# A routed block on one core: the last token tile's router chain put between chunks of expert tiles, and expert tiles that add to the output without waiting for their neighbour

## What is computed

```
t  = tokens(x + involution(layernorm_channels(x)))          # 12544 x 128
n  = layernorm(t)
p, e = top_k(softmax(n @ router_w.T), 2);  p = p / (sum(p) + 1e-9)     # 8 experts, 2 per token
y  = sum over the token's two experts of  p * (silu(n @ w1[e].T) * (n @ w3[e].T)) @ w2[e].T   # hidden 341
out = t + y
```

## Time and profile before

| | |
|---|---|
| median of 3 runs | 1515.86 us (1513.18 to 1517.63) |
| profiled execution | 1514.45 us, its span 1512.6 us |
| busy in the span | PE 1300.8 us, DVE 1074.7, POOL 830.7, ACT 415.9 |
| mean granted TensorE clock | 0.969 of full speed |

### The profile page before, as it was taken

One profiled execution on the slowest core, in us unless ns is written; L12 is line 12 of the kernel. 1 busy time (PEld: TensorE's weight loads), 2 busy tenths in 40 slices (PEclk: granted clock), 3 DMA queues, 4 the chain that ended last, 5 costly groups with the idle time before them and its releaser, 6 DMA issues.

```text
span 1512.6 us, 25000 instructions
## 1 busy us (share of the span) xinstructions
PE 1300.8 (86%) x8596; PEld 1127.5 (75%) x8596; DVE 1074.7 (71%) x2247; ACT 415.9 (27%) x1055; POOL 830.7 (55%) x573
## 2 busy tenths in 40 slices
PE   0598988899999999999999999999999999848871
PEld 0387777788888888888888878888788888737661
DVE  2599899887877878778777887778878778422220
ACT  2112020322323223232232323323232131423330
POOL 1233535357475564756647566475664747464454
PEclk9999999999999999999999999999999999988996
DMA  5001010333334343333433434334333333456662
GB/s 145 13 1 37 20 43 23 88 74 99 74 88 94 74 101 73 86 94 76 99 78 82 96 74 98 79 81 102 67 87 85 83 81 78 108 116 149 147 132 36
DMA packets 91230, 123.37 MB, mean 82 GB/s; under 512 B 13042, under 2 KB 68466, under 8 KB 91104
## 3 DMA queue, kind: packets, MB, share of 16 engines
q1 hardware_dynamic: 54592, 94.95, 21.9%
q0 software_dynamic: 36512, 26.83, 13.0%
HBM read 87.17 MB, written 34.56 MB: 80 GB/s over the span
## 4 chain that ended last, share of the span: by engine, by line
PE 60%; DVE 14%; issue 8%; DMA 7%; ACT 6%; POOL 3%; SPq 1%; POOLq 0%; DVEq 0%; ACTq 0%
PE acc_ps L390 22%; PE kern_ps L468 15%; DVE prod L853 8%; PE bank L500 7%; DMA out<-y_sb,xs 5%; PE hid_ps L492 5%; PE hid_ps L491 5%; PE bank L390 3%; DVE stats_ln L723 3%; POOL out L983 3%; PE bank L421 2%; PE bank L448 1%; ACT L632 1%; DVE x_res L860 1%; ACT rows L583 1%
## 5 line engine op out<-in xcount | busy, mean ns | idle before, releaser
L853 DVE TENSOR_TENSOR prod<-kern_ps,xn 128x896 f32<-128x896 f32 x686 | 733.2, 1084 | 77.8 <-PE kern_ps L468 72.0
L468 PE MATMUL kern_ps<-h_stack,span 98*128 98x448 f32 x1372 | 477.1, 431 | 85.0 <-DVE prod L853 82.7
L390 PE MATMUL acc_ps<-consts_sb,prod 128*128 128x128 f32 x3920 | 545.7, 276 | 0.0
L983 POOL DMA_INDIRECT out<-y_sb,xs x210 | 330.2, 1572 | 335.3 <-ACT y_sb L645 245.1
L390 PEld LDWEIGHTS acc_ps<-consts_sb,prod 128*128 128x128 f32 x3920 | 471.6, 143 | 51.9 <-issue 12.0
L992 POOL TENSOR_TENSOR prod<-prod 128x896 f32<-128x896 f32 x126 | 270.3, 2146 | 183.5 <-DVE prod L853 182.5
L468 PEld LDWEIGHTS kern_ps<-h_stack,span 98*128 98x128 f32 x1372 | 227.9, 194 | 136.8 <-DVE prod L853 120.1
L971 POOL DMA_INDIRECT sorted_x<-rows,dst x196 | 190.7, 973 | 68.3 <-issue 53.7
L632 ACT ACTIVATE silu<-hid_ps 114x256 f32<-114x256 f32 x228 | 87.3, 383 | 418.4 <-PE hid_ps L492 418.2
L873 DVE TENSOR_TENSOR hid<-hid_ps,silu 114x256 f32<-114x256 f32 x228 | 96.2, 422 | 103.0 <-ACT silu L632 102.9
L491 PE MATMUL hid_ps<-xc,w_sb 128*114 128x256 f32 x456 | 137.5, 383 | 1.3
(11 more groups left out here) (93 smaller groups left out, 939.2 us busy)
## 6 DMA issues: line engine op xcount, KB each, us to landing
w_sb<-in_w SPq DMA_DIRECT2D x105, 342.0 KB
w_sb<-in_w SPq DMA_DIRECT2D x105, 192.0 KB, 2.4
xs<-sorted_x SPq DMA_DIRECT2D x105, 130.0 KB, 2.1
x_ln<-in_x SPq DMA_DIRECT2D x14, 448.0 KB, 3.8
x_res<-in_x SPq DMA_DIRECT2D x14, 448.0 KB, 3.5
out<-x_res SPq DMA_DIRECT2D x14, 448.0 KB, 2.5
out<-y_sb,xs POOLq DMA_INDIRECT x210
sorted_x<-rows,dst POOLq DMA_INDIRECT x196, 2.4
```

Source lines behind the costliest of these rows:

```text
L390: return mm(dst, lhsT=src, rhs=eye, is_transpose=True, start=start, stop=True, skip_group_check=True)
L468: i = mm(kern_ps[:, n % 2, h, 0:HALF], span[:, u * C:(u + 1) * C], h_stack[:, m % 2, h * HALF:(h + 1) * HALF], start=True, stop=True)
L853: v.tensor_tensor(tiled(prod[:, n % PRING, :].rearrange("p (h n) -> p h n", h=2)), tiled(kern_ps[:, n % 2, :, 0:HALF]), window(m, u // KS, ...
L983: g.indirect_dma_start(out[:, :], bass.IndirectOffsetOnAxis(ap=xs[:, j % XBUFS, b, C:C + 1].bitcast(U32), axis=0), y_sb[:, j % YBUFS, b, : ...
```

## The change

It has four parts.

1. **Adds.** The counter of landed adds is split in two, by the parity of the tile. In the last stage a tile waits for its neighbour's adds only where the expert changes (or for tiles of no expert), and always for the adds of the tile before that. DVE computes which (`needs`, 3 instructions); POOL reads the number to wait for into a register.
2. **The last tile's chain.** Its normalising, transposes, logits, rank and router steps move forward and are spread over the chunks of tiles 77 to 80; its 14 sends are split 6, 4, 4 behind tiles 78, 79 and 80 in place of 7, 7 behind 78 and 79; SP writes the pads before it waits for the sends; tile 77's loads go ahead of the store of the last residual tile.
3. **The router steps of all tiles** get another order: mask first, then everything that needs the ranks up to `dst`, then the gates. In the slots beside the taps: the exponential goes from u = 20 to u = 25, step 6 (places) to u = 24, `hot_place`, which multiplies two SBUF operands, to u = 25, the cast to `dst` to u = 26, the gates to u = 26 to 28, the table steps to u = 29 to 35, and the sends to u = 29 to 48 (before: 27 to 47). PE may take the shared bank after step 8, not after step 17.
4. **Buffers**: 7 of rows, 5 of `y_sb`, 3 of each weight set.

```
-XBUFS, YBUFS = 6, 4
+XBUFS, YBUFS, WBUFS = 7, 5, 3
...
+        def added(j):
+
+            return 16 * TB * (j // 2 + 1)
...
# load_expert (SP)
-                    for i in (m - 1, m):
-                        sp.wait_ge(s_rows[i % 2], 16 * 2 * NB * (i // 2 + 1))
                     if m == TILES - 1:
                         for e in range(EXPERTS):
...
                         sp.wait_ge(s_pads, 16 * (EXPERTS + 2))
+                    for i in (m - 1, m):
+                        sp.wait_ge(s_rows[i % 2], 16 * 2 * NB * (i // 2 + 1))
...
             load_expert(BESIDE)
+            load_expert(BESIDE + 1)
             store_x1(TILES - 1)
...
# take_bank, rank (PE)
                 elif last == "rank":
-                    pe.wait_ge(s_rt, RT * r + 18)
+                    pe.wait_ge(s_rt, RT * r + 9)
...
# PE after the taps
+                    if (i, c) in ((1, 2), (2, 0)):
+                        channels_of_x1(last, int(i == 2))
+                    if (i, c) == (2, 1):
+                        logits(last)
+                    if (i, c) == (3, 1):
+                        rank(last)
...
# ACT beside the taps
-                    if u == 20:
-                        exponentials(m - 1)
...
+                if u == 25 and 0 <= m - 1:
+                    exponentials(m - 1)
...
# DVE: new step 8 is cnt, 9 hot_place, 10 dst_f, 11 dst, 12 rows<-tok, 13 total (waits for the exponential)
-                    for k in {17: (0,), 18: (1,), 19: (2, 3), 20: (4, 5), 21: (6, 7), 22: (8, 9), 23: (10, 11),
-                              24: (12, 13), 25: (14, 15), 26: (16, 17, 18)}.get(u, ()):
+                    for k in {17: (0,), 18: (1,), 19: (2, 3), 20: (4,), 21: (5,), 24: (6, 7), 25: (8, 9, 10), 26: (11, 12, 13),
+                              27: (14, 15), 28: (16, 17, 18)}.get(u, ()):
...
# DVE after the taps
+                    for k in {(2, 1): (0,), (2, 2): (1, 2), (3, 0): (3, 4, 5), (3, 1): (6, 7, 8, 9, 10, 11),
+                              (3, 2): (12, 13, 14, 15, 16, 17, 18)}.get((i, c), ()):
+                        router_step(last, k)
...
# send (POOL)
-                    pool.wait_ge(s_rt, RT * m + 16)
+                    pool.wait_ge(s_rt, RT * m + 18)
...
# add_to_out (POOL)
-                    if j:
-                        pool.wait_ge(s_added, 16 * TB * j)
+                    if j > stage_tiles(TILES - 1)[0]:
+                        if j == stage_tiles(TILES - 1)[0] + 1:
+                            pool.wait_ge(s_need, 1)
+                        enough = pool.value_load(need_i[0:1, j:j + 1], min_val=added(j - 3), max_val=added(j - 1))
+                        pool.wait_ge(s_added[(j - 1) % 2], enough)
+                        pool.sem_inc(s_enough, 1)
+                    elif j:
+                        pool.wait_ge(s_added[(j - 1) % 2], added(j - 1))
+                    if j >= 2:
+                        pool.wait_ge(s_added[j % 2], added(j - 2))
```

More of the change, by code:

```diff
@@ L231, in build @@
         pad_i = sb("pad_i", [P, EXPERTS], I32)
+        same = sb("same", [P, most])
+        need_i = sb("need_i", [P, FTILES], I32)
         hid = sb("hid", [HC, 2, CPE, T])
@@ L272, in build @@
         s_xs = [sem(f"s_xs{i}") for i in range(XBUFS)]
-        s_w13 = [sem(f"s_w13_{i}") for i in range(2)]
-        s_w2 = [sem(f"s_w2_{i}") for i in range(2)]
+        s_w13 = [sem(f"s_w13_{i}") for i in range(WBUFS)]
+        s_w2 = [sem(f"s_w2_{i}") for i in range(WBUFS)]
         s_xt = sem("s_xt")
@@ L281, in build @@
         s_yout = sem("s_yout")
-        s_added = sem("s_added")
+        s_added = [sem(f"s_added{i}") for i in range(2)]
+        s_need = sem("s_need")
+        s_same = sem("s_same")
+        s_enough = sem("s_enough")
         NCONST = 6
@@ L377, in _ @@
             load_expert(BESIDE)
+            load_expert(BESIDE + 1)
             store_x1(TILES - 1)
-            for j in range(BESIDE + 1, FTILES):
+            for j in range(BESIDE + 2, FTILES):
                 load_expert(j)
@@ L500, in down @@
                         i = mm(dst[:, b * C:(b + 1) * C], hid[:, j % 2, c, b * P:(b + 1) * P],
-                               w2_sb[0:HC, j % 2, c * C:(c + 1) * C], start=b == 0 and c == 0, stop=c == CPE - 1,
+                               w2_sb[0:HC, j % WBUFS, c * C:(c + 1) * C], start=b == 0 and c == 0, stop=c == CPE - 1,
                                skip_group_check=True)
@@ L689, in _ @@
                     q = CPE * i + c
+                    if (i, c) == (1, 0):
+                        norm_x1(last, 0)
                     silus(j, c, kern_ps[:, q % 4 // 2, q % 2, :])
@@ L765, in router_step @@
                 elif k == 5:
-                    i = v.tensor_tensor(mask[:], hot[:, :, 0, :], hot[:, :, 1, :], ALU.add)
+                    i = v.tensor_tensor(diff[:], top[:], top[:, :, 0:1].broadcast_to([P, NB, EXPERTS]), ALU.subtract)
                 elif k == 6:
+                    i = v.tensor_tensor(place[:], lg, repeated(offset[:], 1, NB), ALU.add)
+                elif k == 7:
+                    i = v.tensor_tensor(offset[:], offset[:], bank[:, GT:GT + EXPERTS], ALU.add)
+                elif k == 8:
+                    i = v.tensor_tensor(cnt[:], cnt[:], bank[:, GT:GT + EXPERTS], ALU.add)
+                elif k == 9:
+                    i = v.tensor_tensor(hot_place[:], hot[:], place[:].unsqueeze(2).broadcast_to(each), ALU.mult)
+                elif k == 10:
+                    i = v.tensor_reduce(dst_f[:], hot_place[:], AX, ALU.add)
+                elif k == 11:
+                    i = v.tensor_copy(dst[:, m % 2], dst_f[:])
+                elif k == 12:
@@ L775, in router_step @@
                     i = v.tensor_tensor(gden[:], gden[:], expd[:, :, 0], ALU.add)
-                elif k == 10:
+                elif k == 16:
                     i = v.reciprocal(grec[:], gden[:])
-                elif k == 11:
+                elif k == 17:
                     i = v.tensor_tensor(rows[:, m % 2, :, :, C + 1], expd[:, :, 0:2].rearrange("p b k -> p k b"),
                                         repeated(grec[:], 1, 2), ALU.mult)
[L781 to L792, removed]
@@ L838, in table_step, with needs @@
                 i.then_inc(s_cnt, 1)
+            def needs():
+                a, b = stage_tiles(TILES - 1)
+                q = b - a - 1
+                dve.wait_ge(s_cnt, TS * (TILES - 1))
+                v.tensor_tensor(same[:, 0:q], expert_f[:, 1:q + 1], expert_f[:, 0:q], ALU.is_equal).then_inc(s_same, 1)
+                dve.wait_ge(s_same, 1)
+                v.scalar_tensor_tensor(out=same[:, 0:q], in0=expert_f[:, 1:q + 1], scalar=float(EXPERTS), in1=same[:, 0:q],
+                                       op0=ALU.is_lt, op1=ALU.mult).then_inc(s_same, 1)
+                dve.wait_ge(s_same, 2)
+                v.scalar_tensor_tensor(out=need_i[:, a + 1:b], in0=same[:, 0:q], scalar=-16.0 * TB, in1=need_c,
+                                       op0=ALU.mult, op1=ALU.add).then_inc(s_need, 1)
             def product(n):
@@ L933, in _ @@
                         ln("ln2", last, 3, None, None)
-                    if i == 3:
-                        for k in ((0, 1, 2), (3, 4, 5, 6), (7, 8, 9, 10, 11))[c]:
-                            router_step(last, k)
+                    for k in {(2, 1): (0,), (2, 2): (1, 2), (3, 0): (3, 4, 5), (3, 1): (6, 7, 8, 9, 10, 11),
+                              (3, 2): (12, 13, 14, 15, 16, 17, 18)}.get((i, c), ()):
+                        router_step(last, k)
                     if i == 4:
[L938 to L943, removed]
+                        if c == 0:
+                            v.tensor_tensor(pad_i[:], cnt[:], region8_c, ALU.add)
+                        for k in range((0, 5, 10)[c], (5, 10, TS)[c]):
+                            table_step(last, k)
+                        if c == 2:
+                            needs()
         @block.gpsimd
@@ L1006, in _ @@
                     add_to_out(j, b)
[L1007 to L1012, removed]
+                i = j - BESIDE
+                if 2 <= i <= 4:
+                    for k in range((0, 6, 10)[i - 2], (6, 10, 14)[i - 2]):
+                        send(last, k)
 def kernel(x, L0_conv_reduce_w, L0_conv_reduce_b, L0_conv_span_w, L0_conv_span_b, L0_ffn_router_w,
@@ L1051 @@
         along(np.tile(np.arange(EXPERTS), NB)), along(np.arange(FTILES - stage_tiles(TILES - 1)[0])),
-        along(np.arange(EXPERTS) * REGION)], axis=1))
+        along(np.arange(EXPERTS) * REGION),
+        along([16 * TB * ((j - 1) // 2 + 1) for j in range(stage_tiles(TILES - 1)[0] + 1, FTILES)])], axis=1))
     tok = np.ascontiguousarray(np.arange(TOKENS, dtype=np.uint32).reshape(P, BLOCKS))
```

85 lines of the change are left out of this document (39 added, 46 removed).

## The result

The median falls from 1514.56 us (4 runs) to **1463.45 us** (4 runs, 1462.9 to 1465.73): ratio 0.9663, 95% interval 0.9643 to 0.9682. The forecast was 1468, in a range from 1452 to 1491. The profiled execution took 1463.2 us, its span is 1461.4, 51.2 less than that of before.

A forecast was written before the change was run, and what follows sets the result against it. The chain was taken as mostly PE, with DVE waits, issue and DMA where PE does not end last. From 1514.45 us, 18.3 (adds), 7.6 (hand-over) and 22 (router order) gave 1466.5; the median 1468 us, range 1452 to 1491.

The forecast's parts named there:

- Adds: Last stage, tiles 84 to 104: 11 steps without a wait take 4.4 us, 9 with one 6.2; 18.3 us less.
- SP's 0.72 us: Last stage: POOL's register load was sized by SP's 0.72 us from register load to the DMA load it feeds.
- loads will be denser: Last stage: a step with a wait was taken as 6.2 us, as loads would be denser than before.
- rival 4: Last stage: adds of two tiles hold each other up; at 3.2 us per landing the time is 1532 us; chance 0.04.
- Hand-over: Before the last stage: pads under the sends save 10.3 us, later sends cost 2.7; tile 84's rows 7.6 us earlier.
- tile 81's adds at 1352.6 put tile 82's at 1358.8 at the earliest: Hand-over to the last stage: POOL's adds allow tile 82's add at 1358.8, the rows only at 1360.2.
- Router order: Router passes beside the taps: new step order saves 2.0 us in each of 11 passes, 22 us less.
- rival 1: Router pass: `hot_place` wins the port and POOL waits instead; 10 us more gained, 1458 us; chance 0.22.
- The lead that I counted on: Router pass: DVE's lead swallows about 1.7 us of delay, so PE loses only some 0.8 us behind `hot_place`.
- rival 2: Last stage: adds do not overlap, steps stay 6.1 us, 1486 us; chance 0.12.
- rival 3: Router pass: the new order does nothing, the waits only move, 1490 us; chance 0.13.
- place C: The router pass beside the taps, where DVE's waits cost PE 2.62 us in a pass; 22 us less forecast.

The follow-up runs named there:

- run 5: The kernel after the change, but tiles 85 to 104 load only 8 columns of each weight set: 1454.08 us, ratio 0.96.
- run 7: The kernel after the change, but the last tile's 14 sends stand 7 and 7 behind the adds of tiles 78 and 79: 1470.34 us.
- run 3: The kernel after the change, but `cnt` and `hot_place` stand one slot earlier, at u = 24: 1439.95 us, ratio 0.9506.
- run 1: The kernel after the change, but every tile of the last stage waits for its neighbour's adds again: 1482.66 us, ratio 0.9783.
- run 6: The kernel after the change, but with 6, 4 and 2 buffers as before it: 1458.83 us, ratio 0.9628.
- run 2: The kernel before the change, with only the new router order and its slots: 1495.41 us, ratio 0.9867.
- Run 8: The kernel after the change, with `hot_place` at u = 24 and the table steps ahead of POOL's pair of tap 34: 1442.37 us.

## Why the prediction was right, point by point
**Adds: the sum right, both terms off.** 18.3 us forecast, 19.4 measured. A step without a wait takes 3.70 us, not 4.4: it is POOL's issuing alone, the lower bound. The register load costs nothing, since it runs under the add's issuing; in the chain that ended last its pieces (L1009) stand inside the 1.54 us of L1016:

```profile
1349.65 0.27 POOL out L1016
...
1349.96 0.49 POOLq L1009
```

SP's 0.72 us was the wrong neighbour, for SP had nothing to run it under. A step with a wait takes 6.9 us on the mean, (103.1 - 11 x 3.7) / 9, not 6.2. Here the step "loads will be denser" was sized too small, and rival 4 had its landing right and its cause wrong: landings do stretch to 5.08 us, but run 5 shows that loads do it, not the neighbour's adds. The errors, 7.7 less and 6.5 more, nearly cancel: that this sum came out is luck.

**Hand-over: the rows right, the add 1.7 short.** From the root, tile 84's rows are asked for 7.5 us earlier; the forecast was 7.6. The parts are near: the sends start 0.2 us later where 1 earlier was forecast, the last starts 4.0 later where the end was put 2.7 later, and the way from it to the load is 11.5 shorter for 10.3 (the forecast's own marks, 1352.01 and 1362.6, give 10.6). The step that failed is the next: that "tile 81's adds at 1352.6 put tile 82's at 1358.8 at the earliest", 6.2 us later, so that the rows decide. Tile 81's add took 8.0 us to the next one (1327.74 to 1335.73), and 7.2 to 7.9 in the other runs that keep this code. Tile 82's `y_sb` was ready 1.8 us before its add:

```profile
1333.31 0.62 ACT L656 ACTIVATE y_sb<-acc_ps,xs 128x128 f32<-128x128 f32 x2
```

So POOL's adds decide, as in run 7, where earlier rows brought nothing. Why tile 81's landing is this long stays open: the step is 7.3 us with slivers of weights, but 7.4 in run 3 with full loads. The size of the shortfall is in part that of one execution: in run 1, with the same code up to tile 84, the sends start 27.2 us after the root in place of 28.9, and tile 82's add comes 60.4 after it, 7.8 less than before. From the root to the first send the granted clock was 1.00 there, 0.82 in the kernel after and 0.94 in that of before. That deeper buffers are worth nothing held; that they are free did not quite, run 6.

**Router order: mechanism right, the loss twice as large.** The wait for the exponential goes, the port's wait moves from the cast to `hot_place`, as forecast, and run 3 shows that POOL's pair is its cause. The rule of the Trainium skill that was weighed (SBUF — State Buffer, "Who interferes with whom": two SBUF operands contend with a GpSimd instruction that reads SBUF, the first to issue holds the pair) agrees in these passes: POOL started 0.02 us ahead, and DVE was blocked until it ended. In the kernel before, the starts on record do not bear out its second half. There `done` was held up three times, not once, and each time until a POOL pair ended; in two of them it had itself started some 0.5 us before the pair, while POOL was in a send. DVE and POOL:

```profile
1175.75 2.63 DVE L837 TENSOR_TENSOR done<-begun 128x8 f32<-128x8 f32 x1
```
```profile
1176.24 2.10 POOL L992 TENSOR_TENSOR prod<-prod 128x896 f32<-128x896 f32 x1
```

So it is not shown that `hot_place` would have won the port by starting first, as rival 1 has it. The mis-sized term is what PE loses behind the wait: 1.65 us per pass, not 0.8. The lead that I counted on was not there: two gated chunks wait for their silu at u = 22 and 24, and 2.4 us of `hot_place` and reduce met a lead of some 0.8. That a pass still gained 1.7 us (forecast 2.0) is due to 0.75 us less of PE's busy time, which I had not counted beyond 0.2 for the bank. Three stalls and restarts have become one, which may be it; run 3 takes the last one away and PE is busy 0.24 us less again in a pass (86.87 in place of 87.11). No run settles it, since a matmul's end is modelled.

So eleven passes gave 19 us, not 22. The rest of the 26.3 us is some 3 from the first two passes, left out of the forecast (with pass 3's own gain the kernel is 5.0 us ahead there: PE's loss is at 318.27 before and at 313.29 after), and some 4 from the clock. That the first two, 22 us together, equal the forecast is luck.

Rival 1 falls by the 2.20 us of `hot_place`, rival 2 by the 3.70 us, rival 3 by run 2.

## What to carry to other kernels
The change moved the stall on the shared port from one DVE instruction to another; what removed it was a slot in which POOL runs no pair. So place each DVE step with two SBUF operands, or each cast, by POOL's timetable. One slot was worth some 20 us here by PE's losses, two fifths of the whole change (23.5 us by the medians, which the clock shares). And where transfers that must land gate a chain, look at what their landing sets free: here it freed loads, and without most of these the next landings were shorter.

## What the runs showed of the hardware beyond expectation
The granted clock falls in some passes and not in others that run the same instructions. Run 8 shows it in every second pass: PE waits 0.94 and then 0.91 us for DVE at the start of a token tile, with 1.4 us of matmuls between, and after that it runs at half speed (1.2 GHz in place of 2.4), or doesn't. Two neighbouring passes, windows of 3 us and then the timeline of PE in the one with the fall:

```profile
627.00:630.00 3.00, 1.57 (x10) 1.25 (x11) 3.00 (x10) 0.01 (x1) 0.65 (x1) 1.00 1.06 311
630.00:633.00 3.00, 2.96 (x18) 2.32 (x19) 2.97 (x12) 0.39 (x1) 1.60 (x2) 1.00 0.61 189
...
717.00:720.00 3.00, 1.76 (x10) 1.45 (x11) 3.00 (x12) 0.00 (x0) 0.47 (x1) 0.94 0.95 273
720.00:723.00 3.00, 3.00 (x11) 2.47 (x10) 2.61 (x10) 0.00 (x0) 1.79 (x2) 0.50 0.65 201
723.00:726.00 3.00, 3.00 (x24) 2.83 (x24) 2.27 (x4) 0.38 (x1) 1.82 (x1) 0.99 0.00 0
```
```profile
717.33 0.67 PE L480 MATMUL kern_ps<-h_stack,span 98*128 98x448 f32 x2 [0.94 <-DVE prod L878]
717.84 0.93 PE L402 MATMUL acc_ps<-consts_sb,prod 128*128 128x128 f32 x7
719.68 1.11 PE L480 MATMUL kern_ps<-h_stack,span 98*128 98x448 f32 x2 [0.91 <-DVE prod L878]
720.59 1.05 PE L402 MATMUL acc_ps<-consts_sb,prod 128*128 128x128 f32 x4
```

In the kernel after, the two falls in the ten windows begin at another place, behind PE's loss in the router pass (679.93 and 956.09): the granted clock is 1.00 from 953 to 956 and 0.66 from 956 to 959. Why one pass has a fall and the next has none stays open. A fall costs a pass 1.3 to 1.4 us. In the windows of the kernel before, for instance, against the 93.33 us of the pass shown under place C:

```profile
506.59:601.25 94.66, 89.18 (x602) 78.73 (x602) 75.18 (x160) 28.45 (x72) 57.75 (x40) 0.98 0.38 86
```
